# Moving a spectral product to GpSimd and dropping the mean from five norms

## The reference, cut to what matters

```
z      = layernorm(x)                                  # "norm0"
attn   = top-32 softmax attention over the context     # 4 heads, from LO and M0
a, b   = film_in(attn);   u = a * z + b                # FiLM in front of the filter
y      = irfft(rfft(u) * rfft(K)) + u * D_skip         # long convolution over the 512 tokens
c, d   = film_out(attn);  t = xg + c * y + d           # xg: the normed text
t      = layernorm(t)        -> ffn with W1, W2 -> t'  # "norm1"
x1     = x + tanh(g) * (layernorm(t') * g_out + b_out) # "norm2"
x2     = x1 + tanh(g) * butterfly_ffn(layernorm(x1))   # "norm3"
x3     = x2 + tanh(g) * cross_attention(layernorm(x2)) # "norm4", 16 heads, full softmax
h      = layernorm(x3)                                 # "norm5"
out    = x3 + tanh(g) * sum over the top 2 of 8 experts of
         softmax gate * (silu(h @ Wu) * (h @ Wv)) @ Wo
```

## Time and profile before

| | before |
|---|---|
| median of 3 runs | 363.53 us (363.21 to 364.34) |
| the profiled execution's own time | 362.57 us |
| its span, first to last instruction | 360.7 us |
| mean granted TensorE clock | 0.891 of full speed |
| busy: PE, DVE, ACT, POOL | 274.3, 302.3, 211.4, 161.2 us |

### The profile page before, as it was taken

How to read it: one execution, slowest core, us unless ns; L and a number is a source line. 1 busy time by engine, 2 the same in 40 slices (tenths; PEclk the granted TensorE clock), 3 DMA queues, 4 the chain that set the end, 5 groups by cost and what they waited for, 6 DMA issues and landing times.

```text
span 360.7 us, 6290 instructions
## 1 busy us (share of the span) xinstructions
PE 274.3 (76%) x1848; PEld 183.0 (51%) x1848; DVE 302.3 (84%) x1454; ACT 211.4 (59%) x466; POOL 161.2 (45%) x227
## 2 busy tenths in 40 slices
PE   1261480078859398777989989999999999999985
PEld 0131360057727367555656626767745436663554
DVE  4999999999999989997999999989956745692471
ACT  3767695916402196680335749776676587459661
POOL 2499999966899643564212253511400311001021
PEclk9995556559996789995999999999999999899999
DMA  8990000000000000000000000000000000001001
GB/s 248 387 369 29 2 0 0 1 4 2 2 0 3 0 2 2 0 1 0 2 1 2 1 3 0 1 2 0 2 0 2 2 2 0 2 1 31 0 29 60
DMA packets 6711, 10.74 MB, mean 30 GB/s; under 512 B 660, under 2 KB 4884, under 8 KB 6422
## 3 DMA queue, kind: packets, MB, share of 16 engines
...
...
## 4 chain that ended last, share of the span: by engine, by line
DVE 55%; PE 33%; issue 6%; ACT 3%; POOL 2%; DMA 1%; ACTq 0%; POOLq 0%; DVEq 0%
PE bank L442 31%; DVE R L1117 12%; DVE V L1108 8%; DVE arena L1014 4%; DVE MT L1014 4%; DVE st L1060 3%; DVE HN L1019 3%; DVE arena L1022 2%; DVE mx L1081 2%; DVE X L1014 2%; DVE HN L1014 1%; DVE sm L1043 1%; DVE negm L1019 1%; DVE KT L1348 1%; PE bank L461 1%
## 5 line engine op out<-in xcount | busy, mean ns | idle before, releaser
L757 ACT ACT_TABLE_LOAD x36 | 46.2, 1283 | 4.3 <-DMA pack_kgen<-in_kgen 3.7
L763 ACT ACTIVATE arena<-bank 128x512 f32<-128x512 f32 (+3 forms) x71 | 35.6, 574 | 16.4 <-PE bank L442 10.9
L763 ACT ACTIVATE E<-bank,negm,rs 128x77 f32<-128x77 f32 x64 | 21.3, 414 | 37.7 <-DVE negm L1019 37.7
L1117 DVE MATCH_REPLACE8 R<-V,R 128x77 f32<-128x77 f32 x192 | 40.4, 219 | 0.0
L442 PE MATMUL bank<-arena,pack_dft 128*128 128x256 f32 x128 | 34.0, 425 | 8.1 <-issue 6.2
L442 PE MATMUL bank<-arena 128*32 128x16 f32 (+3 forms) x304 | 16.5, 245 | 25.7 <-issue 25.7
L442 PEld LDWEIGHTS bank<-arena,pack_dft 128*128 128x128 f32 x128 | 27.0, 216 | 16.1 <-issue 8.3
L1397 POOL TENSOR_TENSOR pack_bfly<-pack_bfly,W 128x512 f32<-128x512 f32 x8 | 8.3, 1047 | 56.8 <-DVE pack_bfly L1014 44.8
L1108 DVE MAX8 V<-R 128x8 f32<-128x77 f32 x192 | 31.1, 221 | 0.0
L1489 POOL TENSOR_SCALAR sel<-R 128x308 f32<-128x308 f32 x16 | 18.4, 1148 | 27.0 <-DVE R L1117 25.9
L1081 DVE TENSOR_REDUCE mx<-bank 128x4 f32<-128x308 f32 x64 | 25.4, 469 | 5.5 <-PE bank L442 5.4
...
## 6 DMA issues: line engine op xcount, KB each, us to landing
...
```

The lines of the kernel that those rows point to most:

```text
L757: nc.scalar.add_instruction(mybir.InstLoadActFuncSet(name=nc.get_next_instruction_name(), act_func_set_id=need, ins=[], outs=[]))
L763: return nc.scalar.activation(out, in_, func, **kw)
L1117: nc.vector.match_replace(R8[:, g % 2, r % 2, h, :], V8[:, g % 2, h, r, :], src, NEG)\
```

## The change

It has five parts.

1. A matrix C = I - 1/128 is loaded with the expert weights. New PE steps `s_moe`, `s_cw1` and `s_cwup` multiply it into Wu, Wv, the gate, the second attention's Wq, the gained W1 and the butterfly's up matrix, and ScalarE copies the results back over the weights. A product with a centred weight is the same for x and for x minus its mean.
2. So `norm1`, `norm3` and `norm4` only multiply by rs (one operand in place of two); `norm2` is as before.
3. `norm5` is gone. `lift5` turns X itself; rs5 comes in as the scale of the Silu in `units`, in `top2` (logits are scaled as DVE reads them from the bank; ScalarE's copy of the logits is gone) and in the gate weights.
4. `mix` becomes `mixr` and `mixi`, two steps of seven instructions, one for the real and one for the imaginary half, and all eight of them are in GpSimd's list. `film_pre` on DVE becomes a ScalarE copy of the bank to HN and a GpSimd addition. The second half of `film_out` is a step of its own, `film_add` (DVE). `x1/1`, `x1/2` and `norm4/2` are in GpSimd's list; two memsets of `s_masks` go to GpSimd's `s_row`.
5. All four lists of ORDER are laid out anew. In the new ones, `units`, `top2`, `turn` and `moe_out` of batch 0 and `units` and `top2` of batch 1 stand earlier against batch 3 than before.

The core of the diff:

```diff
-MOE, N_MOE = columns([("gate", NE), ("wu", NE * RE), ("wv", NE * RE), ("wo", 2 * D)])
+MOE, N_MOE = columns([("gate", NE), ("wu", NE * RE), ("wv", NE * RE), ("wo", 2 * D), ("C", P)])
...
     "dve": """
...
+        s_consts s_kgen0 stat0/0 s_qarg s_k0 s_wq s_masks s_parg0 stat0/1 score0/0 s_parg1 s_w1 s_coef nmr0/0
+        stat0/2 stat0/3 score1/0 s_pc0 s_pc1 score2/0 nmr0/1 s_pc2 score3/0 s_pc3 s_qc weigh3/0 score0/1 s_kern1
+        s_kern3 nmr0/2 film_in/0 s_misc s_edge score1/1 nmr0/3 score2/1 score3/1 film_out/0 film_add/0 stat1/0 s_bup
+        norm1/0 weigh3/1 score0/2 ffn_down/0 stat2/0 norm2/0 film_in/1 x1/0 stat3/0 norm3/0 score1/2 fold_down/0
+        stat4/0 norm4/0 scoreA0/0 scoreA1/0 s_v1 scoreA2/0 scoreA3/0 maxT/0 score2/2 film_out/1 film_add/1 stat1/1
+        norm1/1 score3/2 weigh3/2 normA/0 ffn_down/1 stat2/1 wo/0 norm2/1 film_in/2 stat5/0 stat3/1 norm3/1 score0/3
+        fold_down/1 stat4/1 norm4/1 units0/0 top2/0 units1/0 units2/0 units3/0 film_out/2 film_add/2 stat1/2
+        scoreA0/1 scoreA1/1 scoreA2/1 scoreA3/1 norm1/2 maxT/1 score1/3 score2/3 score3/3 weigh3/3 normA/1
+        ffn_down/2 stat2/2 norm2/2 wo/1 film_in/3 stat5/1 stat3/2 norm3/2 units0/1 top2/1 fold_down/2 units1/1
+        stat4/2 units2/1 units3/1 film_out/3 film_add/3 stat1/3 moe_out/0 norm1/3 scoreA0/2 scoreA1/2 scoreA2/2
+        scoreA3/2 maxT/2 ffn_down/3 stat2/3 norm2/3 x1/3 stat3/3 norm3/3 fold_down/3 stat4/3 norm4/3 normA/2
+        moe_out/1 wo/2 stat5/2 scoreA0/3 scoreA1/3 scoreA2/3 scoreA3/3 maxT/3 units0/2 units1/2 units2/2 units3/2
+        top2/2 normA/3 wo/3 stat5/3 top2/3 units0/3 units1/3 units2/3 units3/3 moe_out/2 moe_out/3
...
     "pool": """
...
+        s_row s_ufly pick0/0 s_coef pick1/0 weigh0/0 weigh1/0 pick2/0 s_qal pick3/0 weigh2/0 s_film s_udense
+        weigh3/0 s_dfly pick0/1 mixi/0 weigh0/1 pick1/1 mixr/0 pick2/1 film_pre/0 s_dhigh weigh1/1 pick3/1 s_rows
+        s_dlow s_v1 k1/0 weigh2/1 weigh3/1 x_bias/0 pick0/2 gain/0 mixi/1 k1/1 weigh0/2 mixr/1 pick1/2 film_pre/1
+        x_bias/1 pick2/2 weigh1/2 pick3/2 weigh2/2 weigh3/2 gain/1 x1/1 mixr/2 mixi/2 x_bias/2 film_pre/2 gate0/0
+        gate1/0 k1/2 pick0/3 pick1/3 weigh0/3 pick2/3 weigh1/3 pick3/3 weigh2/3 weigh3/3 x_bias/3 gain/2 x1/2 mixr/3
+        mixi/3 norm4/2 film_pre/3 gate0/1 k1/3 gain/3 gate1/1 gate0/2 gate1/2 gate0/3 gate1/3
...
@@ lift
-                    pe.wait_ge(*normed(tile, b))
+                    if tile == 5:
+                        pe.wait_ge(x_ready["x3"], b + 1)
+                    else:
+                        pe.wait_ge(*normed(tile, b))
...
@@ new PE steps
+                elif step == "s_moe":
+                    pe.wait_ge(loaded["moe"], 16)
+                    w = packs["moe"][0][:, MOE["wu"][0]:MOE["wv"][1]]
+                    mm(claim("moec", 0)[:, :], part("moe", "C"), w).then_inc(s["moe_ready"], 1)
...
+                elif step == "s_cw1":
+                    mm(claim("w1x", 0)[:, :], part("moe", "C"), w1g).then_inc(s["w1_mixed"], 1)
...
+                elif step == "s_cwup":
+                    mm(claim("wupx", 0)[:, :], part("moe", "C"), wupf[:, :]).then_inc(s["wup_ready"], 1)
...
@@ ScalarE, film_pre and units
                     a(AO[:, :], bank("fc", b)[:, :], ACT.Copy).then_inc(s["ao_ready"], 1)
+                    act.wait_ge(s["film_out_ready"], 2 * b + 2)
+                    act.wait_ge(s["filmed"], b + 1)
+                    a(flat(HN[:, b, :, :]), bank("fd", b)[:, :], ACT.Copy).then_inc(s["ao_ready"], 1)
...
+                    act.wait_ge(rs_done, ROOTED.index(("rs5", b)) + 1)
+                    a(SUT[:, tile, :], bank(f"uv{tile}", b)[:, 0:NE * RE], ACT.Silu, scale=rs[:, 5, b, tile:tile + 1]).then_inc(s["silu_ready"], 1)
...
@@ norms on DVE (GpSimd alike)
-                        last = ts(dst[:, b, t, :], src[:, b, t, :], mv[:, tile, b, t, 0:1], rs[:, tile, b, t:t + 1],
-                                  ALU.subtract, ALU.mult)
+                        if tile == 2:
+                            last = ts(dst[:, b, t, :], src[:, b, t, :], mv[:, tile, b, t, 0:1], rs[:, tile, b, t:t + 1],
+                                      ALU.subtract, ALU.mult)
+                        else:
+                            last = ts(dst[:, b, t, :], src[:, b, t, :], rs[:, tile, b, t:t + 1], None, ALU.mult)
...
@@ GpSimd, the product
+                    i, x = int(step == "mixi"), XF
+                    out = YZ[:, i, :, :, :]
+                    linked(tt(m0, x[:, :, 0, :, :], both(H0f[:, i, :, :]), ALU.mult))
+                    chain(tt(m1, x[:, :, 1, :, :], both(H0f[:, 1 - i, :, :]), ALU.mult))
+                    chain(tt(out, m0, m1, ALU.add if i else ALU.subtract))
+                    linked(tt(m0[:, :, 0, :], x[:, :, i, 0, :], H1f[:, 1, :, :], ALU.mult))
+                    chain(tt(m1[:, :, 0, :], x[:, :, 1 - i, 0, :], H1f[:, 0, :, :], ALU.mult))
+                    chain(tt(out[:, :, 1, :], out[:, :, 1, :], m0[:, :, 0, :], ALU.add))
+                    tt(out[:, :, 1, :], out[:, :, 1, :], m1[:, :, 0, :], ALU.subtract if i else ALU.add).then_inc(norms["pool"], 1)
...
+                elif step == "film_pre":
+                    pool.wait_ge(s["ao_ready"], 2 * b + 2)
+                    pool.wait_ge(*normed(0, b))
+                    tt(flat(XG[:, b, :, :]), flat(XG[:, b, :, :]), flat(HN[:, b, :, :]), ALU.add).then_inc(s["shifted_text"], 1)
...
@@ DVE, top2
+                    tt(LG[:, p2, :, 0:NE], bank("logits", b)[:, 0:NT * NE].rearrange("p (t e) -> p t e", t=NT), r5, ALU.mult)\
+                        .then_inc(s["logits_copied"], 1)
...
+                    chain(tt(gsum[:, p2, :], gsum[:, p2, :], rs[:, 5, b, :], ALU.mult))
```

More of the change, by code:

```diff
@@ new lines @@
+        s_k0 s_m0 score0/0 score1/0 score2/0 s_vw score3/0 score0/1 s_w1 s_kern0 s_kern1 vw/0 attnT/0 s_kern2
+        s_kern3 film_in/0 vw/1 s_freq dft/0 score1/1 s_moe film_pre/0 s_t1 score2/1 s_cw1 s_wup score3/1 s_bup
+        idft/0 s_cwup k1/0 s_t2 lift1/0 score0/2 ffn_up0/0 ffn_up1/0 ffn_down/0 attnT/1 k1/1 s_wdn film_in/1 vw/2
+        dft/1 score1/2 film_out/0 lift3/0 fold_up0/0 fold_up1/0 fold_down/0 vw/3 film_pre/1 lift4/0 q/0 scoreA0/0
+        scoreA1/0 s_v1 scoreA2/0 scoreA3/0 score2/2 idft/1 maxT/0 keyA0/0 keyA1/0 film_out/1 keyA2/0 score3/2
@@ new lines @@
+        mixA0/0 mixA1/0 lift1/1 ffn_up0/1 ffn_up1/1 mixA2/0 ffn_down/1 wo/0 attnT/2 normA/0 film_in/2 film_pre/2
+        dft/2 lift3/1 score0/3 fold_up0/1 k1/2 lift5/0 fold_up1/1 fold_down/1 logits/0 units0/0 units1/0 units2/0
+        lift4/1 units3/0 idft/2 q/1 scoreA0/1 scoreA1/1 film_out/2 scoreA2/1 scoreA3/1 score1/3 turn0/0 maxT/1
+        turn1/0 lift1/2 keyA0/1 score2/3 k1/3 keyA1/1 mixA0/1 keyA2/1 score3/3 ffn_up0/2 ffn_up1/2 mixA1/1 mixA2/1
+        ffn_down/2 wo/1 attnT/3 normA/1 film_in/3 lift5/1 dft/3 units0/1 lift3/2 logits/1 units1/1 units2/1
@@ new lines @@
+        fold_up0/2 fold_up1/2 fold_down/2 film_pre/3 units3/1 idft/3 film_out/3 lift4/2 moe_out/0 q/2 scoreA0/2
+        lift1/3 scoreA1/2 scoreA2/2 ffn_up0/3 ffn_up1/3 scoreA3/2 ffn_down/3 maxT/2 keyA0/2 keyA1/2 keyA2/2 mixA0/2
+        mixA1/2 lift3/3 turn0/1 turn1/1 fold_up0/3 fold_up1/3 fold_down/3 normA/2 mixA2/2 moe_out/1 lift4/3 wo/2 q/3
+        scoreA0/3 lift5/2 scoreA1/3 scoreA2/3 scoreA3/3 units0/2 units1/2 units2/2 units3/2 maxT/3 keyA0/3 logits/2
+        normA/3 keyA1/3 keyA2/3 mixA0/3 mixA1/3 mixA2/3 turn0/2 wo/3 turn1/2 lift5/3 logits/3 units0/3 units1/3
@@ L89 @@
+        units2/3 units3/3 moe_out/2 turn0/3 turn1/3 moe_out/3
     """,
     "act": """
[L91 to L94 removed]
@@ L100 @@
[L100 to L103 removed]
+        s_kgen0 s_qlag s_plag rs0/0 s_trig s_m0 s_qsin score0/0 s_psin0 s_pexp s_cols score1/0 s_vw rs0/1 s_qexp
@@ new lines @@
+        score0/3 k1/2 lift5/0 rs4/1 units0/0 top2/0 units1/0 units2/0 lift4/1 units3/0 q/1 rs1/2 score1/3 maxT/1
+        turn0/0 lift1/2 turn1/0 keyA0/1 k1/3 score2/3 keyA1/1 keyA2/1 score3/3 ffn_up0/2 ffn_up1/2 normA/1 rs2/2
+        attnT/3 rs3/2 lift5/1 dft/3 rs5/1 lift3/2 units0/1 units1/1 units2/1 top2/1 fold_up0/2 fold_up1/2 rs4/2
+        film_pre/3 units3/1 lift4/2 rs1/3 q/2 lift1/3 ffn_up0/3 ffn_up1/3 maxT/2 rs2/3 keyA0/2 keyA1/2 rs3/3 keyA2/2
+        lift3/3 turn0/1 fold_up0/3 turn1/1 fold_up1/3 rs4/3 normA/2 lift4/3 q/3 lift5/2 rs5/2 units0/2 units1/2
@@ L104 @@
+        maxT/3 units2/2 units3/2 keyA0/3 keyA1/3 keyA2/3 top2/2 normA/3 turn0/2 lift5/3 turn1/2 rs5/3 top2/3
+        units0/3 units1/3 units2/3 units3/3 turn0/3 turn1/3
     """,
     "dve": """
-        s_kgen0 s_wq s_consts s_masks s_qarg stat0/0 s_k0 s_parg0 stat0/1 s_parg1 score0/0 s_coef s_w1 score1/0
-        stat0/2 s_edge score2/0 s_pc0 nmr0/0 s_pc1 score3/0 score0/1 s_qc s_pc2 weigh3/0 s_bup s_pc3 score1/1
-        film_in/0 s_kern1 s_kern3 score2/1 film_pre/0 mix/0 score3/1 score0/2 film_out/0 nmr0/1 stat1/0 weigh3/1
```

227 lines of the change are left out of this document (101 added, 126 removed).

## The result

The changed kernel took 381.67 us (median, 380.56 to 383.91), the kernel before 363.58 us beside it: a ratio of 1.052 [1.047, 1.057]. Forecast was 346 us. The profiled execution took 381.82 us for a span of 379.9.

What follows compares the result with a forecast made beforehand. DVE's late hand-over bounds the kernel until about 260 us, then PE. `lift1/3` at 262 plus 75.5 us gives 337.5, raised to 343.3 for PE idleness; plus 1.9 and 1.0 gives 346 us, range 335 to 358.

Steps and rivals of the forecast that it cites:

- DVE's and GpSimd's work: Busy time of both engines: DVE falls from 302 to about 261 us, GpSimd rises from 161 to about 211.
- Norms beside GpSimd: DVE norm steps meeting GpSimd operations: zero in the sum; 7.5 us, with some six additions, kept for a rival.
- the walk to `score3/3`: DVE's list up to the last top-k step: 228 - 27 + 17 + 9, ending near 227 us.
- work term: DVE up to `score3/3`: loses 27 us of work, gains 17 us of steps taken forward.
- term of waits: DVE up to `score3/3`: 16 us of open waits for the product, less roughly 6.5 us idled there before.
- The check from PE's side: Whole span from PE's work and idleness: middle idle 13 to 14 us, not 7, so 343 to 344 us.
- Rival 1: Waits for GpSimd, by longer products or port conflicts, take back 10 to 15 us: 356 us (352 to 362), chance 0.24.
- The centring: Added PE work, three 512-column products and two small ones: about 3.3 us, standing while PE waits for DVE's first batches.
- The scaled `top2`: Two tiny operations added on DVE in each `top2`, with a wait each: 2 us in all, between 1 and 4.
- The tail: From `lift1/3` to the end on PE: 90.7 us less 15.2 us of steps taken forward, leaving 75.5 us.
- Rival 4: Slower: GpSimd's line in front delays batch 1's attention by more than 20 us: 366 to 370 us, chance 0.07.
- signs of being wrong: PE still idle 28 us in the middle, DVE waiting over 10 us on GpSimd's picks, or `attnT/1` later than before.

Runs made afterwards that it cites:

- e4: The changed kernel with its new order lists, but the front of each list as in the kernel before: 380.43 us, ratio 1.045 [1.040, 1.051].
- g1: The changed kernel with dummy PE products filling gaps where PE waits, list otherwise unchanged: 376.82 us, ratio 1.036 [1.029, 1.043].

## Why the prediction was wrong

- **DVE's and GpSimd's work** was sized about right: DVE 269.6 us for 261, GpSimd 205.6 for 211, half a product 6.8 us for 7.1. The one-operand norm was taken at 0.5 us and is 0.88: a saving of 0.2 a step, not 0.6.
- **Norms beside GpSimd** were put at zero "since the norms have not shown it". They had: five steps of the kernel before took 1.42 to 2.05 us beside GpSimd where 1.09 to 1.11 is the undisturbed time, 3.6 us too much in all. In the changed kernel the excess over 0.88 us is about the same, 3.4 us, so it explains no loss by its sum. The Trainium skill's page SBUF — State Buffer, section Who interferes with whom, lists `tensor_scalar` among the operations that can enter a two-port mode and then contend with GpSimd; the rows of both forms agree with it, though no run here isolates the mode.
- **The failing step** is the walk to `score3/3`: near 227 us forecast, 262.9 measured. Its work term was nearly right: 215.7 us busy before - 27 + 17 = 205.7 forecast, 211.8 measured. Its term of waits failed: 16 us, all of them for the product, where the idle time was 12.4 before and should have come to some 22, and came to 51.1. It left PE out. DVE waits 29.3 us for PE's banks (4.3 before), among them those of the second attention's scores, which PE, at half clock and full, hands over late (6.14 us and three times 1.1 us from 160 to 176 us); GpSimd then idles 18.2 us for DVE. The waits for the product itself are not there: in the changed kernel DVE had none ahead of `film_out/0` and `film_out/2`, where 8 us each were forecast, and 1.25 us ahead of `film_out/3`, where 14 were.
- **The check from PE's side failed in two of four terms.** Forecast: 273.6 busy + 50 idle in front + 13.5 in the middle + 7 behind = 344. Measured: 288.3 + 64.2 + 15.2 + 12.2 = 379.9. The middle's idleness, which I thought the boldest of them, was right. PE's work was not: I let the clock give back 4 us, and it took. Counted over windows of 2 us and the whole trace, busy time times (1 - granted clock) is 20.0 us before and 28.4 after. These 8.4 us are more than half of the 14.0 us by which PE's busy time grew; beyond 80 us alone it is 10.5 before and 26.0 after. I took "busy at a lower clock" for a gift of DVE's lateness. Filling PE's pauses removes much of it (half-clock work of 45 us to 24, and of 18 to 2), so it hangs on them; but the changed kernel has no more of them. From 80 to 260 us either kernel has 13 pauses of 0.5 us or more, 27.8 us in all before and 15.1 after. Why fewer idle us brought more half-clock work is not shown. The front's idleness was measured, but e4 shows that restoring the old front gives almost nothing.
- **The product** alone, in the old lists, turns 18 us of saved DVE work into a loss of 2.7%, 9.9 us, by waits at `film_out` in batches 0 and 3 and at `film_in/2`. Rival 1 named these waits but took them off a gain, at 356 us; no rival had them as a net loss.
- **The centring** was priced at 3.3 us of PE work. In the pause it costs 3.5 us, so that price was right for its work; ahead of `ffn_up/0`, where the old lists with all edits had it, it costs some 6.6 us.
- **The scaled `top2`** was priced at 2 us of small operations. In the old lists it holds PE's bank of the logits until DVE and ScalarE have done it, some 6 us; I named no wait for it.
- **The tail** was about right: 75.5 us forecast from `lift1/3`, 79.6 measured.
- **Rival 4** had the right sign, and with 366 to 370 us came nearest, by the wrong mechanism: `attnT/1` came 5.6 us later than before, not 20. Of the signs of being wrong only this one came; the other two, PE idle 28 us in the middle and DVE more than 10 us behind GpSimd's picks, did not (15.2 us, and 7.1 up to `score3/3`).

What stays open: how the remaining 13 us between g1 and the kernel before split among the product, `film_pre` and the centring in the new lists. In the old ones it is measured term by term, and that the same terms hold in the new ones is argued, not shown.
